# Slot feed-forward of a two-layer image and text model: weight units loaded in the order of their use, second bias read once and copied by GpSimd

## What is computed

```python
y = jnp.einsum('btd,bst->bsd', xn, dispatch_w)
y = jnp.einsum('sio,bsi->bso', fc1_weight, y) + fc1_bias
y = jax.nn.gelu(y, approximate=False)
y = jnp.einsum('sio,bsi->bso', fc2_weight, y) + fc2_bias
out = jnp.einsum('bsd,bst->btd', y, combine_w)
```

## Time and profile before

| | |
|---|---|
| median of three runs | 1104.42 us (1103.48 to 1104.73) |
| the profiled execution | 1107.96 us |
| span of its trace | 1105.9 us |
| busy in the span | PE 854.4, PE weight load 704.6, DVE 603.4, ACT 432.1, POOL 398.7 us |
| the slot feed-forward | 404 to 608 us of the span: 204 us |
| in it | PE 86.59, DVE 27.91, ACT 22.16, POOL 0 us busy; mean DMA share 0.86, 317 GB/s |

### The profile page before, as it was taken

How to read it: one execution, slowest core, us unless ns; L and a number is a source line. 1 busy time by engine, 2 the same in 40 slices (tenths; PEclk the granted TensorE clock), 3 DMA queues, 4 the chain that set the end, 5 groups by cost and what they waited for, 6 DMA issues and landing times. The chain is left out here.

```text
span 1105.9 us, 23004 instructions
## 1 busy us (share of the span) xinstructions
PE 854.4 (77%) x7560; PEld 704.6 (64%) x7561; DVE 603.4 (55%) x1401; ACT 432.1 (39%) x1022; POOL 398.7 (36%) x390
## 2 busy tenths in 40 slices
PE   3599999999977980444445599889157999999994
PEld 2477887878667960222223467667156999999994
DVE  1657777777753610111111668887794656555552
ACT  5245555545554320000001047764442444444442
POOL 1345444454301300000000026674275565555552
PEclk9689999999955575666668789999557999999998
DMA  9490000000000039989994190000432333332331
GB/s 286 133 409 1 1 0 0 0 0 0 1 1 2 2 113 364 368 361 355 338 336 114 32 399 2 0 0 1 132 79 61 51 50 51 52 50 49 53 53 19
DMA packets 38126, 119.42 MB, mean 108 GB/s; under 512 B 7538, under 2 KB 28564, under 8 KB 33716
## 3 DMA queue, kind: packets, MB, share of 16 engines
q1 hardware_dynamic: 25108, 104.40, 25.6%
q0 software_dynamic: 10848, 12.67, 7.1%
q10 hardware_dynamic: 2112, 1.57, 1.0%
HBM read 105.87 MB, written 11.14 MB: 106 GB/s over the span
## 5 line engine op out<-in xcount | busy, mean ns | idle before, releaser
L1029 PE MATMUL psum<-flat,m_yT 64*32 64x384 f32 x624 | 48.0, 671 | 104.3 <-issue 103.0
L1646 POOL DMA_INDIRECT out_h<-x_ys,idx x55 | 87.3, 1587 | 98.9 <-ACT x_ys L1671 79.3
L1770 PE MATMUL psum<-w_pairs,x_h_hi 128*128 x330 | 101.7, 370 | 1.1 <-DVE x_h_lo L1698 1.1
L1029 PEld LDWEIGHTS psum<-flat,m_yT 64*32 64x32 f32 x624 | 17.7, 143 | 130.0 <-issue 130.0
L986 DVE COPY f_hid<-psum 128x384 f32<-128x384 f32 x16 | 8.9, 558 | 148.7 <-PE psum L1029 148.7
L1222 POOL MEMSET b_ones<- 96x96 f32 x1 | 0.2, 178 | 242.8 <-POOLq L122 242.8
L1772 PE MATMUL psum<-w_pairs,x_h_lo 128*128 x330 | 82.8, 251 | 0.0
L1698 DVE TENSOR_TENSOR x_h_lo<-psum,x_h_hi 128x384 fp32r<-128x384 f32 x110 | 56.3, 553 | 38.8 <-ACT x_h_hi L1667 36.8
L464 POOL TENSOR_TENSOR a_kb<-a_qk,a_hmask 96x576 f32<-96x576 f32 x64 | 72.2, 1147 | 6.2 <-ACT a_qk L497 6.2
L622 PE MATMUL psum<-a_kb,a_qk 96*96 96x384 f32 (+1 forms) x256 | 67.7, 407 | 0.0
L550 DVE TENSOR_REDUCE a_mx<-psum 96x12 f32<-96x1152 f32 x32 | 43.3, 1354 | 41.8 <-PE psum L622 41.8
(11 more groups left out here) (274 smaller groups left out, 2460.2 us busy)
## 6 DMA issues: line engine op xcount, KB each, us to landing
flat<-in_slot_w SPq DMA_DIRECT2D x27, 2304.0 KB, 21.7
ring_last<-in_slot_w SPq DMA_DIRECT2D x5, 2304.0 KB, 27.9
flat<-in_moe_w SPq DMA_DIRECT2D x1, 10752.0 KB, 29.7
flat<-in_x_patches SPq DMA_DIRECT2D x4, 1536.0 KB, 14.6
out_h<-flat SPq DMA_DIRECT2D x1, 2304.0 KB, 12.2
xtab<-flat SPq DMA_DIRECT2D x4, 576.0 KB, 4.0
m_y<-in_fc_b SPq DMA_DIRECT2D x1, 1536.0 KB, 18.4
m_y<-f_y2g ACTq DMA_DIRECT2D x16, 96.0 KB
```

The costliest lines, as they stand in the source:

```text
L1029: mm = pe.matmul(b_h[n][r][B * c:B * (c + 1), :], g.yT[rows, k, SC * gr + c, :], w1[c // 2][rows, c % 2, k, n * N2:(n + 1) * N2], start=(k ...
L1646: pool.indirect_dma_start(out=A["out"][:, :], out_offset=bass.IndirectOffsetOnAxis(ap=g.idx[:, i:i + 1], axis=0), in_=ys[:, i % 2, :], in_ ...
L1770: pe.matmul(b_y[u % 2], h_hi[:, k, :], g.w_pairs[:, :, k, bass.ds(e, 1), :].rearrange("p two a d -> p two (a d)"), start=(k == 0), stop=False)
```

## The change

It does two things. The units are loaded in the order in which PE uses them: `ORDER` lists pairs of parts, group 0's first matrices, then for each group the first matrices of the next group and the second matrices of this one; `TURN` is its inverse, and PE's waits look up the buffer in it. And the second bias is read once, 48 KB into a new tile `b2` (named `f_b` in the profile, like the first bias), ahead of all units; GpSimd then copies it to all 32 samples with one instruction, and waits for its end.

```diff
+def use_order():
+    pairs = [(0, 0)]
+    for gr in range(NGR):
+        if gr + 1 < NGR:
+            pairs.append((gr + 1, 0))
+        pairs.append((gr, 2))
+    return [(gr, part + i) for gr, part in pairs for i in range(2)]
+
+ORDER = use_order()
+TURN = {unit: u for u, unit in enumerate(ORDER)}
 
 def load_unit(sp, A, g, u):
-    gr, part = u // PER, u % PER
+    gr, part = ORDER[u]
...
+            sp.dma_start(b2[NS:2 * NS, :], A["fc2_b"]).then_inc(s_b2, 16)
             for u in range(NU, NGR * PER):
-                gr, part = (u - NU) // PER, (u - NU) % PER
+                gr, part = ORDER[u - NU]
                 if part < 2:
                     sp.wait_ge(s_h1, 2 * gr + 2)
                 else:
                     sp.wait_ge(s_y2p, 2 * gr + part - 1)
                 load_unit(sp, A, g, u)
-                if u == NU:
-                    sp.dma_start(g.y2[NS:2 * NS, :, :], A["fc2_b"].unsqueeze(1).broadcast_to([NS, B, D])).then_inc(s_b2, 16)
-            sp.wait_ge(s_b2, 16)
+
+        @block.gpsimd
+        def _(pool):
+            pool.wait_ge(s_b2, 16)
+            pool.tensor_copy(g.y2[NS:2 * NS, :, :], b2[NS:2 * NS, :].unsqueeze(1).broadcast_to([NS, B, D])).then_inc(s_b2w, 1)
+            pool.wait_ge(s_b2w, 1)
...
-            def landed(u):
+            def landed(gr, part):
+                u = TURN[gr, part]
                 pe.wait_ge(g.s_ring[u % NU], 16 * (u // NU + 1))
+                return g.ring[u % NU]
```

More of the change, by code:

```diff
@@ L926, in slot_ffn @@
         y2g = sb("y2g", [128, 2, 2, D])
+        b2 = sb("b2", [2 * NS, D])
+        s_b2w = sem("b2w")
         s_b1, s_b2, s_h1, s_hid_a, s_hid_v, s_hTp, s_hb, s_gelu, s_y2p, s_y2s = (
@@ L1013, in _ @@
         def _(pe):
-            def landed(u):
+            def landed(gr, part):
+                u = TURN[gr, part]
                 pe.wait_ge(g.s_ring[u % NU], 16 * (u // NU + 1))
+                return g.ring[u % NU]
             def first(gr):
-                landed(PER * gr)
-                landed(PER * gr + 1)
-                w1 = [g.ring[(PER * gr + i) % NU].rearrange("p (c k f) -> p c k f", c=2, k=KQ) for i in range(2)]
+                w1 = [landed(gr, i).rearrange("p (c k f) -> p c k f", c=2, k=KQ) for i in range(2)]
                 if gr >= 1:
@@ L1046, in second @@
                 for r in range(2):
-                    landed(PER * gr + 2 + r)
+                    w2 = landed(gr, 2 + r).rearrange("p (c k d) -> p c k d", c=SC, k=FC)
                     pe.wait_ge(s_gelu, 3 * gr + 2 + r)
@@ L1050, in second @@
                         pe.wait_ge(s_y2s, gr)
-                    w2 = g.ring[(PER * gr + 2 + r) % NU].rearrange("p (c k d) -> p c k d", c=SC, k=FC)
                     for k in range(FC):
```

## The result

The changed kernel takes 1093.82 us (median of four runs, 1093.19 to 1093.96), the kernel before beside it 1104.58 us (four runs, 1103.48 to 1110.73). The ratio is 0.9879, with a 95% interval of 0.9857 to 0.9901. By the medians that is 10.8 us less, by the ratio 13.4 us, where the prediction had 10.

The account below looks back on a forecast made before the run. It took four DMA engines, which carry all `put`s besides their share of the weights, to bound the stage. Bias -9.1 and restarts -1 made -10 us: 1104.42 to 1094.4 us, range 1087 to 1101.5.

Parts of the forecast that it names:

- the full stream: Rival, 6%: the `put`s are not the limit, the stage is as long as its weights; -44 us, 1060.
- The bias: Removing the large bias DMA, at 411 to 422 in the stage, saves 9.1 us, bounds 3.7 and 11.
- It comes off the path in full: The bias DMA lay on all engines with no pause before it to hide in, so all 9.1 us go.
- on the four it changes nothing in the sum: The new unit order leaves the four `put` engines' work unchanged; 1 us gained, between 0 and 5.7.
- two restarts: Weights restarting onto running `put`s, at 533 to 538 and 561 to 566, lose 2.5 and 3.2 us.
- the check of the sum: The four engines' work in the stage, added up as 200.3 us, ends at 605.6, within 1 us of measured.
- the lone packets: The 1380 `put` packets sent without weights beside them, at 34.7 per us, take 39.8 us.
- slower: Rival, 10%: after the weights, leftover `put`s form a serial chain costing 12.5 us; +2.5 us in all, 1107.
- The `put` packets under the stream: Sign: beside the weights they go at 5.5 per us; clearly more than 6 would refute the mechanism.
- no idle time: The four `put` engines are never idle in the stage; finding them idle in a pause would refute the mechanism.
- DVE's new wait: Sign: `y_copy` waits for `put` landings, tens of us in total, and PE's `second` waits for DVE.
- POOL's copy: GpSimd's bias copy takes 12.6 us, up to 25, covered by over 160 us of the stage.

Follow-up runs that it names:

- hbm_after: The changed kernel with the `put`s sent to a scratch array in HBM, read back by one 1536 KB DMA at the end; 1072.12 us, 0.9679 of the kernel before.
- hbm_bias: The kernel before, old order kept, with the bias copied by GpSimd and the `put`s sent by way of HBM; 1081.17 us, 0.9777 of the kernel before.
- after_again: The changed kernel, unaltered, measured a second time; 1093.02 us, 0.9869 of the kernel before.

## Why the prediction was right, and where it was not

**The time and the bound** were right. Four engines hold the stage: moving or halving the `put`s gives 21 to 22 us, and the shares of 0.27 in the pause that is left show them again. Rival "the full stream" needed this not to be so; `hbm_after` looks like it, and took a second edit.

**The bias** came off at 8.5 us alone (predicted 9.1, bounds 3.7 to 11) and 8.3 us beside spread `put`s, both times in the old order. "It comes off the path in full" didn't hold for the change as a whole: on top of the new order it was 3.5 to 4.6 us.

**The step that failed: "on the four it changes nothing in the sum", taken as 1 with a bound of 5.7.** Alone the order is worth 9.5 us, 8.4 with spread `put`s, and 0.9918 - 0.9869 = 0.0049, 5.4 us, on top of the bias; only the last is inside the bound. Three things were wrong in it. First, I priced only two restarts. The trace before has three more, by stretch:

```profile
452.00:455.00 3.00, 2.65 (x44) 1.94 (x32) 1.74 (x3) 0.00 (x0) 0.00 (x0) 1.00 0.98 291
478.00:482.00 4.00, 3.47 (x64) 2.60 (x54) 1.92 (x4) 0.14 (x1) 0.00 (x0) 1.00 0.84 255
505.00:511.00 6.00, 3.08 (x52) 2.31 (x44) 2.44 (x4) 1.67 (x3) 0.00 (x0) 1.00 0.96 294
```

Against 426 GB/s they lose 0.9, 1.6 and 1.9 us, which with 2.5 and 3.2 makes 10.1, ten times the 1 us that I had put into the sum. The kernel after has one restart, 530 to 536 at 269 GB/s, 2.2 us. The difference, 7.9, is of the size of the gain. (In two of these stretches, from 478 and from 530, the first microsecond still belongs to the pause: their first units are issued at 478.12 and 530.51. That takes about 0.9 us from each side of the difference.) Second, `hbm_bias` shows that late requests and the thin stream behind them cost 5 or 6 us even where no `put` lags, and a longer piece of PE's work stands behind the last unit. Third, the check of the sum misled me. It closed within 1 us while it left out some 9 us of slow restarts, so another of its terms must have been as much too large: the likeliest is that of the lone packets, 1380 at 34.7 per us. The kernel after shows 44.8 per us in one stretch and 40 in another (below); at these they take 30.8 or 34.5 us instead of 39.8. That points the right way, by 5 to 9 us, and is no proof. A sum that closes did not show that its terms were right. How the order's worth divides between restarts, late requests and the tail in the kernel as it is, these runs don't settle.

**Why the total was still right**: the range was wide enough, and the middle of it was partly luck. Put one upon the other, the two parts are worth 8.5 and then 5.4 us, 13.9, and I had 9.1 and 1. By the ratios the change gave 13.4 and 14.5 us; the 10.8 of the first medians, which so nearly meets my 10, rests on four runs of the kernel before with a median of 1104.58, where the later batches have 1106.6 to 1107.9. I had neither the order's gain nor the overlap of the two gains, and these two errors have opposite signs: 8.5 + 9.5 = 18 us apart, 13.4 to 14.5 together. The likely place of the 4 to 5 us is the mechanism of the rival "slower", in a small size. When the weights are in, the end waits for a serial chain. The timeline of the kernel after:

```profile
572.83 0.56 DVE L1022 COPY f_y2g<-psum 128x384 f32<-128x384 f32 x1 [19.16 <-DMA m_y<-f_y2g]
573.41 1.18 ACTq L988 DMA_DIRECT2D m_y<-f_y2g  x2
...
575.89 6.94 PE L1073 MATMUL psum<-flat,f_hT 128*32 128x192 f32 x96 [11.83 <-ACT f_hT L982]
...
583.48 1.15 ACTq L988 DMA_DIRECT2D m_y<-f_y2g  x2
...
593.36 0.93 PE L1100 MATMUL psum<-m_y,m_combT 128*96 128x192 f32 x2 [10.53 <-PEq L928]
```

The `y_copy` of group 6 waits for a landing. Behind it on DVE stands the `add_bias` of group 7, behind that ACT's `gelu` (574.64), and `second(7)` waits for that. Then `second(7)` itself is slow: it takes 6.94 us, where the last `second` before took 4.11. PE had had nothing to do for 11.83 us, and runs at a granted clock of about half, the lower of its two levels (1.2 of 2.4 GHz):

```profile
576.00:582.00 6.00, 6.00 (x81) 4.21 (x84) 0.00 (x0) 0.31 (x1) 0.00 (x0) 0.53 0.26 30
```

In the kernel before the clock was 1.00 from 588 to 600. So the four engines run dry before the last pair (the share of 0.06 at 581), for about 3 us, and the 2.8 us that `second` takes longer are nearly as much. In `after_again` the same `second` took 5.42 us, and the share from 582 to 585 was 0.13. That is a cost of about 3 us, not the 12.5 of that rival; this reading comes from the traces, no run isolates it. The 12.5 had a wrong reading in it too. I took 10 us as the time of a lone pair, but when that pair was issued at 596.74 the one before was not yet through: 317 packets went from 598 on, and a pair has 264. The last pair of the kernel after is alone, from 583 to 593:

```profile
q10 hardware_dynamic: 264, 0.20, 19.4%
```

Its packets go from about 584.5 to 591.1, 40 per us, and it is through 7.6 us after its issue.

**What was to be seen.** The `put` packets under the stream: 113 in 19 us, 5.9 per us, as said. `first(2)` starts at 418.30 (419 said). Weights ended before 575: 381 GB/s in 557 to 567, then 83 until 571. Alone, the queue of the `put`s from 570 to 580:

```profile
q10 hardware_dynamic: 448, 0.33, 26.5%
```

44.8 per us, where the first 8 us of the tail before had 34.1. From 580 to 590 there are 291, with the dry 3 us among them. So one rate for all lone packets was too simple, and 34.7 likely too low. The four engines idle for these 3 us, which by my own sign speaks against "no idle time"; it holds in the pause at 518 and not in the tail. DVE's new wait came as said, but PE's `second` then waits for ACT, not directly for DVE; that is below. POOL's copy was far under cover and shorter than all my estimates:

```profile
400.50 5.30 POOL L966 COPY m_y<-f_b 64x6144 f32<-64x6144 f32 x1 [13.34 <-DMA f_b<-in_fc_b]
```

## What to carry to other kernels

A pause in which few bytes move but the DMA share stays at a round fraction is a busy minority of engines: look which small DMA has few partitions at one end, and spread it, even by a detour through HBM. Load a ring in the order of use even where it doesn't seem to hold the bound: here each stop was followed by 3 to 6 us at 155 to 294 GB/s, at a busy share of 0.84 to 1.04 that doesn't show it. Count this worth with its limits: the order gave 9.5 us alone and 5.4 on top of the bias. A long wait of PE had a second price here: the matmuls behind it ran at about half the clock, 6.94 us for 4.11. A sum of terms that closes on the measured time is a check of the total, not of a term; a change priced by one of its terms wants that term tested by itself.

## What the runs showed that I had not expected

ACT is held at the issue of a `put`. In the kernel after the timeline has three pairs of issues that take 12.84 to 15.18 us and one of 6.26, all where earlier `put`s are still on their way under the stream; in the kernel before each of the eight pairs takes 1.15 to 1.78 us. One of the three, with what follows it:

```profile
511.61 13.49 ACTq L988 DMA_DIRECT2D m_y<-f_y2g  x2
525.14 1.67 ACT L982 ACTIVATE f_hT<-f_hT 128x512 f32<-128x512 f32 x3 [38.65 <-issue]
...
526.39 6.10 PE L1073 MATMUL psum<-flat,f_hT 128*32 128x192 f32 x96 [29.08 <-ACT f_hT L982]
```

A pair of issues that takes 1.15 us at 583.48 took 13.49, and 0.81 with the `put`s spread in `hbm_after`. That a full queue is the cause is inferred from this. The `gelu` behind them on ACT came that much later, and PE's `second` behind it. But the hold is not all of PE's wait, which began at 497.3: until 511.0 DVE was waiting for the landing, with the `add_bias` that the `gelu` needs queued behind its `y_copy`. Of these 29.1 us about 14 are the landing's and 13.5 ACT's hold. The other wait in the 40.9 us, the 11.83 before `second(7)`, has no long hold in it: it lasts until the `y_copy` of 572.83 could start, 8.8 us, and then for the work behind that.

GpSimd's copy with a broadcast source ran at 5.30 us for 6144 elements for each partition, 0.86 ns each, where the row has 2.05 on 192 elements. If the short one goes at the same rate, 165 of its 394 ns are its elements and the rest is a fixed cost; that is an estimate from these two rows.

The read back of 1536 KB in `hbm_after`, into 64 partitions with nothing beside it, is far slower than the weights' rows:

```profile
564.00:570.00 6.00, 0.00 (x0) 0.00 (x0) 0.00 (x0) 0.00 (x0) 0.00 (x0) 0.50 1.13 246
```

246 GB/s at a full share, against 429 for the units in the same kernel. The share of 1.13 comes from one DMA on one queue, so a share over 1 doesn't need packets of two queues, as I had put it above.
